# A two-layer pair-product kernel on one Trainium2 core: a new order of the slots, and the products with x1 in two row tiles of 64 rows, evicted two quarters at a time

## Chip, cores and metric

The kernel runs on one core of a Trainium2 chip. The metric is the device time of one execution in microseconds (us); lower is better. The time before is the median of three runs.

## What is computed

The input `x` has 2048 samples of 39 fields with 16 features each. There are two layers. Layer one is `x1[b,h,d] = sum over i,j of x[b,i,d] * x[b,j,d] * W0[i,j,h]` with 128 outputs h, layer two is `x2[b,h,d] = sum over i,j of x[b,i,d] * x1[b,j,d] * W1[i,j,h]`. The output is both layers summed over d, 256 numbers for each sample. The core of the reference:

```python
for W in (W0, W1):
    Hk = xk.shape[1]
    Wr = W.reshape(m, Hk, W.shape[-1])
    xk = jnp.einsum('bid,bjd,ijh->bhd', x0, xk, Wr)
    outs.append(xk)
return jnp.sum(jnp.concatenate(outs, axis=1), axis=-1)
```

## The kernel before, in words

**Numbers.** Every operand of a matmul is held as a high part in fp32r, and a low part that is the rest. A product of two such numbers is three matmuls that add into the same bank: high by high, low by high, high by low. ScalarE (ACT) makes the high parts by a Copy, VectorE (DVE) and GpSimd (POOL) make the low ones by a subtraction.

**Groups and chunks.** The 2048 x 16 columns are cut into 64 groups of 512 columns (32 samples). Eight groups are a chunk, so there are 8 chunks. The index `g` is a group, `gi` its place in its chunk, `j` the chunk. Chunk 0 and the last are written out, those between run in a loop of two chunks. Even and odd chunks store `gh` and `gl` in two different layouts, so that chunk j can overwrite the block that chunk j-1 has been read from.

**Layer one of a group.** SyncE (SP) loads x as the left factor (`xs`, 256 KB) and six slots of right factors (`xr`, 1536 KB, one transfer), each into one of two buffers. The products of slots 0, 2, 3, 5 are DVE's (L551), those of 1, 4 POOL's (L639). ACT rounds each to `fh` (L415), DVE (L555) or POOL (L644) subtracts to `fl`. PE adds three matmuls of 512 columns for each slot into `acc` (`main`, L329 to L331), and a seventh, FULL, for squares (L324). The products and roundings of group g+1 are made in the period in which PE works on group g.

**Layer two.** `x1_out` copies `acc` to SBUF (L436), `fill_turn` transposes it by four 128-column operations (L339), and L447 and L564 split the result into `x1th` and `x1tl`. The small matrix x1 x x of each sample is made by `g_tile` (L342 to L356) for a quarter (8 samples, 128 rows of (sample, feature)): the moving operand `xbd` is block diagonal, 8 samples by 40 columns, so each of three matmuls has 128 rows and 320 columns. Seven eighths of `xbd` are zeros. Two banks of `pg` take turns. ACT evicts each quarter as `gh` (L455, 128x320), DVE then as `gl` (L569). At the end of 8 groups `final` (L358 to L370) contracts 39 rows of gh and gl with `w1` in 39 x 3 matmuls of 256 columns; they are spread over the next chunk by `EARLY_ROWS` and `LATE_ROWS`.

**Order on PE in a period** (`chunk`, L372): early rows of `final`, quarters 2 and 3 of group g-2's place (`gi - 2`), slots 0, 1, 2, the transposes of g-1, slots 3, 4, late rows of `final`, slot 5, quarters 0 and 1 of g-1, FULL. In the first group of a chunk there are no rows of `final`, in the second 5, in the others 6 (5 in the last).

**Order on SP** (L273 to L293): when the products 4 and 5 of g are made, xs and xr of g+2; then `blocks`: eight small transfers that write the block diagonal (L264, SBUF to SBUF), after quarter 3 of g-2 is done; every second group the pair rows `xp`; then `xdr` of g+2. SP issues all transfers, one after another in program order. In chunk 0 it also loads w1 in 10 pieces into `outs`, each after POOL has split the one before.

**Start.** `w0a_raw` and `w0b_raw` lie in the second `xr` buffer, so `xr` of group 1 is loaded after the weights are split (L303, L304). PE waits for all weights (L395) before its first matmul.

Of the kernel before, what the change touches and what calls it, by code (L numbers as in the profile page):

```python
# [18 lines left out]
NT = 6  # L19
# [8 lines left out]
BQ = P // D  # L28
GB = GC // D
# [14 lines left out]
NW = 4  # L44
PIECES = -(-M // NW)
EARLY_ROWS = (0, 0, 2, 3, 3, 3, 3, 3)
LATE_ROWS = (0, 5, 3, 3, 3, 3, 3, 2)


def rows_of(gi, late):  # L50

    r0 = sum(EARLY_ROWS[:gi]) + sum(LATE_ROWS[:gi])
    if late:
        r0 += EARLY_ROWS[gi]
    return range(r0, r0 + (LATE_ROWS if late else EARLY_ROWS)[gi])


def pieces_of(gi):

    extra = PIECES - CB  # L60
    return range(gi + min(gi, extra), gi + 1 + min(gi + 1, extra))
# [41 lines left out]
def build(nc, xa, xb, xd, xpairs, w0a, w0b, w1, ident, out):  # L103
    with ExitStack() as ctx:
# [28 lines left out]
        xbd = sb("xbd", [P, 2, NQ, 2, BQ, MI], F32R)  # L133
# [4 lines left out]
        pg = ps("pg", [P, 2, GC])  # L138
# [3 lines left out]
        xr_flat = xr[:, 1, :, :].rearrange("p s c -> p (s c)")  # L142
        nw0 = len(ORDER) * H

        w0a_raw = xr_flat[:, 0:nw0]
        w0b_raw = xr_flat[:, nw0:2 * nw0]

        w0_in = sem("w0_in")
# [4 lines left out]
        xbd_zero = sem("xbd_zero")  # L153
        w1_in = sem("w1_in")
# [3 lines left out]
        xr_in = [sem("xr_in0"), sem("xr_in1")]  # L158
# [24 lines left out]
        outs_dma = sem("outs_dma")  # L183

# [19 lines left out]
        def wait_high(eng, g, t):  # L204
            eng.wait_ge(high_done, NT * g + t + 1)
# [7 lines left out]
        def g_at(g_buf, odd, gi, q):  # L213


            bs = slice(q * BQ, (q + 1) * BQ)
# [9 lines left out]
        def g_psum(odd, q):  # L226
            if odd:
                return pg[:, q % 2, 0:BQ * MI].rearrange("p (b i) -> p i b", b=BQ)
            return pg[:, q % 2, 0:BQ * MI].rearrange("p (b u r) -> p u r b", b=BQ, r=IB)
# [4 lines left out]
        def _(sp):  # L234
# [3 lines left out]
            def load_right(j, gi):  # L238
                sp.dma_start(xr[:, gi % 2, :, :], xb[CB * j + gi]).then_inc(xr_in[gi % 2], 16)
# [6 lines left out]

            def w1_load(p):
                n = min(NW, M - NW * p)
                if p:
                    sp.wait_ge(w1_ready, p)  # L250
                sp.dma_start(outs[:, :, :].rearrange("p a b -> p (a b)")[:, 0:n * H],
                             w1[:, NW * p * H:(NW * p + n) * H])\
                  .then_inc(w1_in if p < PIECES - 1 else outs_dma, 16)

            def blocks(g, gi, first):
                sp.wait_ge(xd_low, g + 1)
                if first and gi < 2:
                    sp.wait_ge(xbd_zero, 1)
                else:
                    sp.wait_ge(g_done, NQ * (g - 1))  # L260
                s = gi % 2
                for b in range(BQ):
                    rows = slice(D * b, D * b + D)
                    sp.dma_start(xbd[rows, s, :, :, b, :].rearrange("p q s i -> p (q s) i").bitcast(F32),  # L264
# [8 lines left out]
            def chunk(j, first, last):  # L273
                for gi in range(CB):
                    g = CB * j + gi
                    if not (last and gi + 2 >= CB):
                        wait_product(sp, g, 4)
                        wait_product(sp, g, 5)
                        load_x(j, gi + 2)
                        load_right(j, gi + 2)  # L280
                    blocks(g, gi, first)
                    if gi % 2 == 0 and not (last and gi + 2 >= CB):
                        sp.wait_ge(sq_ready, CP * j + gi // 2 + 1)
                        load_pair(CP * j + gi // 2 + 1)
                    if not (last and gi + 2 >= CB):
                        sp.wait_ge(xd_low, g + 2)
                        load_xd(g + 2)
                    if first:
                        for p in pieces_of(gi):
                            if p + 1 < PIECES:  # L290
                                w1_load(p + 1)
                    if gi == CB - 1 and not first:
                        send(j - 1)  # L293

            sp.dma_start(w0a_raw, w0a).then_inc(w0_in, 16)
            sp.dma_start(w0b_raw, w0b).then_inc(w0_in, 16)
            load_x(0, 0)
            load_right(0, 0)
            load_xd(0)
            load_pair(0)  # L300
            load_x(0, 1)
            sp.dma_start(idn[:, :], ident).then_inc(ident_in, 16)
            sp.wait_ge(w0_ready, 2)  # L303
            load_right(0, 1)  # L304
            w1_load(0)
            sp.wait_ge(xd_low, 1)
            load_xd(1)
            chunk(0, True, False)
            with sp.Fori(1, NCH - 1) as j:
                chunk(j, False, False)  # L310
            chunk(NCH - 1, False, True)
# [4 lines left out]
        def _(pe):  # L316
            def main(j, gi, t, fresh):
                g = CB * j + gi
                if t == 0 and not fresh:
                    pe.wait_ge(x1_ready, g)  # L320
                if t == FULL:
# [12 lines left out]
            def fill_turn(g, fresh):  # L334
                pe.wait_ge(x1_ready, g + 1)
                if not fresh:
# [5 lines left out]
            def g_tile(j, gi, q, fresh):  # L342
# [399 lines left out]
```

## Time and profile before

| | |
|---|---|
| median of 3 runs | 660.48 us (659.22 to 661.25) |
| the profiled execution | 658.78 us |
| its span | 657.0 us (so 1.78 us lie around it) |
| mean granted TensorE clock | 0.948 of 2.4 GHz |
| PE matmul busy | 573.5 us, 87% |
| ACT, DVE, POOL busy | 481.6, 477.2, 472.6 us (73, 73, 72%) |
| share of the 16 DMA engines | 68.6%, mean 226 GB/s |

The profile is one execution. Engine rows give busy time, and the idle time before a group of instructions with what ended it. SP's transfers stand as `SPq` rows whose time is that of the issue alone; an issue is not counted as busy. Starts and times in timelines are in us; PE rows overlap, since the end of a matmul lies after the start of the next, so what a matmul costs in a packed stretch is the distance between two starts.

### The profile page before, as it was taken

The numbers are of one execution on the slowest core, as the hardware profiler recorded it, in microseconds if no ns is written. First come the engines' busy times: TensorE is split into PE (matmuls) and PEld (weight loads), VectorE is DVE, ScalarE is ACT, GpSimd is POOL, SyncE is SP. The second block draws the span as 40 slices with busy tenths as digits, with TensorE's granted clock in tenths as the row PEclk, the third lists the DMA queues.
The fourth block names the chain that finished last, engine by engine and source line by source line (L and its number), as shares of the span: only waits on it lengthen the run. The fifth ranks groups of instructions, "written<-read, shape, count | busy, mean of one in ns | idle before, by whom it ended". The sixth has DMA issues, their size and how long they took to land.

```text
span 657.0 us, 13101 instructions
## 1 busy us (share of the span) xinstructions
PE 573.5 (87%) x3176; PEld 498.3 (76%) x3176; DVE 477.2 (73%) x804; ACT 481.6 (73%) x982; POOL 472.6 (72%) x407
## 2 busy tenths in 40 slices
PE   0458778999979998899979997999989999899978
PEld 0247666888868987688968896789968898689968
DVE  4527777788887787688886886878886888878730
ACT  3448787878877887678876887778887788778830
POOL 5668987778866887578875888578876788778700
PEclk9878898899989999799988999899998999999989
DMA  5757888668886687677775776867787677876310
GB/s 217 275 159 233 266 265 260 225 201 269 263 279 190 223 265 269 194 239 254 250 255 196 262 247 204 261 231 219 251 272 250 198 243 257 280 251 216 93 26 17
DMA packets 109081, 148.23 MB, mean 226 GB/s; under 512 B 77648, under 2 KB 86096, under 8 KB 100816
## 3 DMA queue, kind: packets, MB, share of 16 engines
q1 hardware_dynamic: 109008, 147.37, 68.6%
q8 instruction: 32, 0.52, 0.3%
q14 instruction: 41, 0.34, 0.2%
HBM read 134.74 MB, written 2.10 MB: 208 GB/s over the span
## 4 chain that ended last, share of the span: by engine, by line
PE 57%; DVE 14%; issue 11%; ACT 8%; DMA 6%; POOL 1%; ACTq 1%; SPq 0%; DVEq 0%
PE acc L329 9%; PE acc L330 9%; PE acc L331 9%; DMA xr<-xb_dram 5%; PE pg L354 5%; PE fin L366 5%; PE fin L367 5%; PE fin L368 4%; PE pg L355 4%; PE pg L356 4%; DVE fl L555 3%; DVE gl L569 3%; ACT gh L455 3%; PE turn L339 3%; DVE fp L551 2%
## 5 line engine op out<-in xcount | busy, mean ns | idle before, releaser
L644 POOL TENSOR_TENSOR fl<-fs,fh 128x512 fp32r<-128x512 f32 x192 | 256.7, 1337 | 67.0 <-ACT fh L415 66.8
L569 DVE TENSOR_TENSOR gl<-pg,gh 128x320 fp32r<-128x320 f32 x256 | 114.5, 486 | 110.5 <-ACT gh L455 109.6
L329 PE MATMUL acc<-fh,w0h 128*128 128x512 f32 x384 | 163.7, 426 | 25.0 <-DVE w0q L615 16.4
L639 POOL TENSOR_TENSOR fs<-xr,xs 128x512 f32<-128x512 f32 x128 | 163.7, 1301 | 8.7 <-DMA xr<-xb_dram 6.0
L415 ACT ACTIVATE fh<-fp 128x512 fp32r<-128x512 f32 x192 | 115.0, 599 | 63.5 <-DVE fp L551 37.5
L330 PE MATMUL acc<-fh,w0l 128*128 128x512 f32 x384 | 156.7, 408 | 0.0
L331 PE MATMUL acc<-fl,w0h 128*128 128x512 f32 x384 | 156.1, 406 | 0.0
L555 DVE TENSOR_TENSOR fl<-fp,fh 128x512 fp32r<-128x512 f32 x192 | 132.1, 688 | 28.1 <-ACT fh L415 25.8
L415 ACT ACTIVATE fh<-fs 128x512 fp32r<-128x512 f32 x192 | 120.1, 626 | 24.3 <-PE acc L331 19.7
L551 DVE TENSOR_TENSOR fp<-xl,xr 128x512 f32<-128x512 f32 x192 | 127.4, 694 | 13.6 <-DMA xr<-xb_dram 10.0
L354 PE MATMUL pg<-xbd,x1th 128*128 128x320 f32 x256 | 88.0, 344 | 51.4 <-DVE gl L569 32.5
L455 ACT ACTIVATE gh<-pg 128x320 fp32r<-128x320 f32 x256 | 101.2, 431 | 31.3 <-PE pg L356 24.9
L354 PEld LDWEIGHTS pg<-xbd,x1th 128*128 128x128 f32 x256 | 50.5, 197 | 69.9 <-DVE gl L569 42.8
L329 PEld LDWEIGHTS acc<-fh,w0h 128*128 128x128 f32 x384 | 76.5, 199 | 35.5 <-DVE w0q L615 16.4
L366 PE MATMUL fin<-gh,w1h 128*128 128x256 f32 x312 | 89.0, 285 | 1.1 <-DVE gl L569 1.1
L331 PEld LDWEIGHTS acc<-fl,w0h 128*128 128x128 f32 x384 | 75.8, 197 | 18.3
L367 PE MATMUL fin<-gh,w1l 128*128 128x256 f32 x312 | 88.9, 285 | 0.0
L368 PE MATMUL fin<-gl,w1h 128*128 128x256 f32 x312 | 88.6, 284 | 0.0
L330 PEld LDWEIGHTS acc<-fh,w0l 128*128 128x128 f32 x384 | 76.6, 199 | 10.0
L355 PE MATMUL pg<-xbd,x1th 128*128 128x320 f32 x256 | 82.5, 322 | 0.0
L356 PE MATMUL pg<-xbd,x1tl 128*128 128x320 f32 x256 | 82.5, 322 | 0.0
L648 POOL TENSOR_TENSOR xdhl<-xdr,xdhl 128x160 fp32r<-128x160 f32 x64 | 34.1, 533 | 66.6 <-ACT xdhl L443 66.6
(35 smaller groups left out, 730.6 us busy)
## 6 DMA issues: line engine op xcount, KB each, us to landing
xr<-xb_dram SPq DMA_DIRECT2D x64, 1536.0 KB, 7.5
xs<-xa_dram SPq DMA_DIRECT2D x64, 256.0 KB, 2.9
xbd<-xdhl SPq DMA_DIRECT2D x512, 20.0 KB, 3.4
xp<-xpairs_dram SPq DMA_DIRECT2D x32, 256.0 KB, 2.7
xdr<-xd_dram SPq DMA_DIRECT2D x64, 80.0 KB, 2.4
outs<-w_dram SPq DMA_DIRECT2D x9, 256.0 KB, 2.9
out_dram<-outs SPq DMA_DIRECT2D x8, 256.0 KB, 2.8
xr<-w0a_dram SPq DMA_DIRECT2D x1, 512.0 KB, 3.3
```

The lines of the kernel that those rows point to most:

```text
L329: nc.tensor.matmul(acc[:, :], w0h[:, t, :], fh[:, t, :], start=t == 0, stop=False)
L330: nc.tensor.matmul(acc[:, :], w0l[:, t, :], fh[:, t, :], start=False, stop=False)
L331: nc.tensor.matmul(acc[:, :], w0h[:, t, :], fl[:, t, :], start=False, stop=False)\
L354: nc.tensor.matmul(o, x1th[:, q, :], xh, start=True, stop=False)
L366: nc.tensor.matmul(o, w1h[:, i, :], h, start=i == 0, stop=False)
L367: nc.tensor.matmul(o, w1l[:, i, :], h, start=False, stop=False)
L415: nc.scalar.activation(fh[:, t, :], f_at(t), COPY).then_inc(high_done, 1)
L551: nc.vector.tensor_tensor(f_at(t), xl[:, :], xr[:, gi % 2, t, :], ALU.mult).then_inc(prod_dve, 1)
L555: nc.vector.tensor_tensor(fl[:, t, :], f_at(t), fh[:, t, :], ALU.subtract).then_inc(low_dve, 1)
L569: nc.vector.tensor_tensor(g_at(gl, odd, gi, q), g_psum(odd, q), g_at(gh, odd, gi, q), ALU.subtract).then_inc(g_low, 1)
L639: nc.gpsimd.tensor_tensor(f_at(t), xr[:, gi % 2, t, :], xs[:, gi % 2, :], ALU.mult)\
L644: nc.gpsimd.tensor_tensor(fl[:, t, :], f_at(t), fh[:, t, :], ALU.subtract).then_inc(low_pool, 1)
```

## The change

- **Row tiles.** `g_pair` takes the place of `g_tile`. A quarter's 128 rows are cut into two halves of 64 rows (4 samples each), and `xbd` has 4 blocks rather than 8, so each matmul has 64 rows and 160 columns. The two halves write different banks of `pg`. A pair of quarters is 2 x 3 x 2 = 12 matmuls, and `pg` (2 banks) holds one pair, with samples 64 columns apart. The next pair waits until the one before is evicted.
- **Eviction.** L455 and L569 become two instructions of 128x640 a group, where there were four of 128x320.
- **PE's order:** pair 0 of g-2, slots 0 to 2, pair 1 of g-2, transposes of g-1, slots 3 to 5, five rows of `final` (four in a chunk's first group, which are the last rows of the chunk before the previous one), FULL. The orders of ACT, DVE and POOL follow.
- **SP's order:** `blocks` first, then `xr` of g+3 in three transfers of two slots (512 KB each), each as soon as the products that read those slots are made, and `xs` of g+3.
- **Start.** w0 comes in two parts, into other places, and PE waits for each when it first needs it. w1 is copied in HBM to `w1_copy` (7 pieces), then loaded to `w1l` (7 pieces) and split in place.

The host permutes the samples of x accordingly. The diff, cut to what the text speaks of:

```diff
-NW = 4
+NR = 2
+RT = P // NR
+BR = BQ // NR
+BU = 2 * BQ
+NPAIR = NQ // 2
+HIGH = (0, 1, 2, 4, 3, 5)
+W0_PART = 4
+W0_FROM = {0: 1, W0_PART: 2, FULL: 3}
+NW = 6
-EARLY_ROWS = (0, 0, 2, 3, 3, 3, 3, 3)
-LATE_ROWS = (0, 5, 3, 3, 3, 3, 3, 2)
+def rows_of(s):
+    return range(IB * (s - 1), min(IB * s, M))
...
-        xbd = sb("xbd", [P, 2, NQ, 2, BQ, MI], F32R)
+        xbd = sb("xbd", [P, 2, NQ, 2, BR, MI], F32R)
-        pg = ps("pg", [P, 2, GC])
+        pg = ps("pg", [P, BU, GC // BR // 2])
...
-            def load_right(j, gi):
-                sp.dma_start(xr[:, gi % 2, :, :], xb[CB * j + gi]).then_inc(xr_in[gi % 2], 16)
+            def load_right(j, gi, u):
+                sp.dma_start(xr[:, gi % 2, 2 * u:2 * u + 2, :], xb[CB * j + gi][:, 2 * u:2 * u + 2, :])\
+                  .then_inc(xr_in[u][gi % 2], 16)
...
+            def w1_move(p):
+                sp.dma_start(w1_copy[:, piece(p), :], w1[:, piece(p), :]).then_inc(w1_moved, 16)
...
-            def chunk(j, first, last):
+            def chunk(j, first, second, last):
                 for gi in range(CB):
                     g = CB * j + gi
-                    if not (last and gi + 2 >= CB):
-                        wait_product(sp, g, 4)
-                        wait_product(sp, g, 5)
-                        load_x(j, gi + 2)
-                        load_right(j, gi + 2)
-                    blocks(g, gi, first)
+                    blocks(g, gi, first, last and gi == CB - 1)
+                    if more3:
+                        wait_product(sp, g + 1, 0)
+                        wait_product(sp, g + 1, 1)
+                        load_right(j, gi + 3, 0)
+                    if gi % 2 == 0 and more2:
                         sp.wait_ge(sq_ready, CP * j + gi // 2 + 1)
                         load_pair(CP * j + gi // 2 + 1)
+                    if more3:
+                        wait_product(sp, g + 1, 3)
+                        load_right(j, gi + 3, 1)
+                    if first and gi < PIECES:
+                        w1_load(gi)
+                        if gi + 1 < PIECES:
+                            w1_move(gi + 1)
+                    if more3:
+                        wait_product(sp, g + 1, 4)
+                        load_x(j, gi + 3)
+                        wait_product(sp, g + 1, 5)
+                        load_right(j, gi + 3, 2)
+                    if more2:
                         sp.wait_ge(xd_low, g + 2)
                         load_xd(g + 2)
...
-            def g_tile(j, gi, q, fresh):
+            def g_pair(j, gi, u, fresh):
                 g = CB * j + gi
                 s = gi % 2
-                if q == 0:
+                if u == 0:
                     pe.wait_ge(x1t_low, g + 1)
                     pe.wait_ge(xbd_in[s], 16 * BQ * nth(j, gi))
-                if not (fresh and q < 2):
-                    pe.wait_ge(g_low, NQ * g + q - 1)
-                o = pg[:, q % 2, 0:BQ * MI]
-                xh = xbd[:, s, q, 0, :, :].rearrange("p b i -> p (b i)")
-                xlo = xbd[:, s, q, 1, :, :].rearrange("p b i -> p (b i)")
-                nc.tensor.matmul(o, x1th[:, q, :], xh, start=True, stop=False)
-                nc.tensor.matmul(o, x1th[:, q, :], xlo, start=False, stop=False)
-                nc.tensor.matmul(o, x1tl[:, q, :], xh, start=False, stop=True).then_inc(g_done, 1)
+                if not fresh:
+                    pe.wait_ge(g_low, NPAIR * g + u)
+                for q in (2 * u, 2 * u + 1):
+                    for n, (left, part) in enumerate(((x1th, 0), (x1th, 1), (x1tl, 0))):
+                        for t in range(NR):
+                            rows = slice(RT * t, RT * t + RT)
+                            b0 = BQ * t + BR * (q % 2)
+                            o = pg[:, b0:b0 + BR, 0:MI]
+                            last = nc.tensor.matmul(o, left[rows, q, :],
+                                                    xbd[rows, s, q, part, :, :],
+                                                    start=n == 0, stop=n == 2)
+                last.then_inc(g_done, 1)
...
+                    if not (first and gi < 2):
+                        g_pair(j, gi - 2, 0, first and gi == 2)
+                    main(j, gi, 0, fresh)
+                    main(j, gi, 1, fresh)
+                    main(j, gi, 2, fresh)
+                    if not (first and gi < 2):
+                        g_pair(j, gi - 2, 1, False)
+                    if not fresh:
                         fill_turn(g - 1, first and gi == 1)
...
+                    main(j, gi, 3, fresh)
+                    main(j, gi, 4, fresh)
+                    main(j, gi, 5, fresh)
+                    if gi and not first:
+                        final(j - 1, not odd, rows_of(gi), second)
+                    if not gi and not (first or second):
+                        final(j - 2, odd, rows_of(CB), False)
+                    main(j, gi, FULL, fresh)
```

## Rows read from the trace of the kernel before

**Rows 1.** The page: busy time of each engine, its share of the span
```profile
PE 573.5 (87%) x3176; PEld 498.3 (76%) x3176; DVE 477.2 (73%) x804; ACT 481.6 (73%) x982; POOL 472.6 (72%) x407
```

**Rows 2.** PE timeline (start, us, what): transposes of groups 0, 8 and 63
```profile
38.98 1.05 PE L339 MATMUL turn<-idn,x 128*128 128x128 f32 x4
...
122.04 0.60 PE L339 MATMUL turn<-idn,x 128*128 128x128 f32 x4
...
631.37 0.60 PE L339 MATMUL turn<-idn,x 128*128 128x128 f32 x4
```

**Rows 3.** Busy time by stretch: bounds, length, engines, PEclk, DMA share, GB/s
```profile
38.98:122.04 83.06, 63.24 (x282) 51.70 (x280) 57.66 (x99) 62.42 (x128) 65.32 (x56) 0.89 0.78 248
...
301.17:318.64 17.47, 17.47 (x107) 15.72 (x106) 14.24 (x26) 14.78 (x31) 14.37 (x12) 1.00 0.80 263
```

**Rows 4.** PE timeline of one group in the packed stretch, 301.17 to 309.92
```profile
301.17 0.60 PE L339 MATMUL turn<-idn,x 128*128 128x128 f32 x4
301.53 0.48 PE L329 MATMUL acc<-fh,w0h 128*128 128x512 f32 x1
301.84 0.40 PE L330 MATMUL acc<-fh,w0l 128*128 128x512 f32 x1
...
303.00 0.28 PE L366 MATMUL fin<-gh,w1h 128*128 128x256 f32 x1
...
304.08 0.39 PE L329 MATMUL acc<-fh,w0h 128*128 128x512 f32 x1
...
304.78 0.31 PE L354 MATMUL pg<-xbd,x1th 128*128 128x320 f32 x1
...
305.66 0.39 PE L324 MATMUL acc<-sq,w0q 128*128 128x512 f32 x1
...
309.92 0.60 PE L339 MATMUL turn<-idn,x 128*128 128x128 f32 x4
```

**Rows 5.** PE timeline at the start of a chunk: the waits
```profile
181.35 0.41 PE L354 MATMUL pg<-xbd,x1th 128*128 128x320 f32 x1 [0.63 <-DVE gl L569]
181.60 0.31 PE L355 MATMUL pg<-xbd,x1th 128*128 128x320 f32 x1
...
188.90 0.41 PE L354 MATMUL pg<-xbd,x1th 128*128 128x320 f32 x1 [1.79 <-DVE x1tl L564]
```

**Rows 6.** SP timeline: its issues in one group of the packed stretch
```profile
308.07 5.30 SPq L264 DMA_DIRECT2D xbd<-xdhl  x8
313.56 0.45 SPq L245 DMA_DIRECT2D xdr<-xd_dram  x1
314.36 0.34 SPq L236 DMA_DIRECT2D xs<-xa_dram  x1
314.88 0.33 SPq L239 DMA_DIRECT2D xr<-xb_dram  x1
316.81 1.23 SPq L264 DMA_DIRECT2D xbd<-xdhl  x2
```

**Rows 7.** SP timeline in chunk 0: the eight block transfers
```profile
36.66 5.92 SPq L264 DMA_DIRECT2D xbd<-xdhl  x8
```

**Rows 8.** Timeline of the start: first product, first matmul, FULL of group 0, group 1
```profile
10.62 0.70 DVE L551 TENSOR_TENSOR fp<-xl,xr 128x512 f32<-128x512 f32 x1 [4.35 <-DMA xr<-xb_dram]
...
22.72 1.30 DVE L551 TENSOR_TENSOR fp<-xl,xr 128x512 f32<-128x512 f32 x2 [4.62 <-DMA xr<-xb_dram]
...
34.97 0.80 PE L329 MATMUL acc<-fh,w0h 128*128 128x512 f32 x1 [8.61 <-ACT x L436]
```

**Rows 9.** ACT and DVE timelines: evictions of two quarters, and 512 columns
```profile
305.85 0.74 ACT L455 ACTIVATE gh<-pg 128x320 fp32r<-128x320 f32 x2
...
308.81 0.60 ACT L415 ACTIVATE fh<-fp 128x512 fp32r<-128x512 f32 x1 [0.34 <-PE acc L331]
...
636.82 0.49 DVE L569 TENSOR_TENSOR gl<-pg,gh 128x320 fp32r<-128x320 f32 x1 [1.28 <-ACT gh L455]
...
310.83 0.69 DVE L555 TENSOR_TENSOR fl<-fp,fh 128x512 fp32r<-128x512 f32 x1
```

More of the change, by code:

```diff
@@ L43, with piece @@
 ORDER = (*range(NT), FULL, FULL)
-NW = 4
-PIECES = -(-M // NW)
-EARLY_ROWS = (0, 0, 2, 3, 3, 3, 3, 3)
-LATE_ROWS = (0, 5, 3, 3, 3, 3, 3, 2)
[L50 to L61, printed above, removed]
+HIGH = (0, 1, 2, 4, 3, 5)
+NU = NT // 2
+W0_PART = 4
+W0_FROM = {0: 1, W0_PART: 2, FULL: 3}
+NW = 6
+PIECES = -(-M // NW)
+def rows_of(s):
+    return range(IB * (s - 1), min(IB * s, M))
+def piece(p):
+    return slice(NW * p, min(NW * p + NW, M))
 def pair_slots():
@@ L297, in _ @@
-            load_x(0, 0)
-            load_right(0, 0)
+                    if gi == 2 and not (first or second):
+                        send(j - 2)
+            w0_load(0)
+            load_x(0, 0)
+            load_right(0, 0, 0)
+            w0_load(1)
+            load_right(0, 0, 1)
+            load_right(0, 0, 2)
+            load_pair(0)
             load_xd(0)
-            load_pair(0)
             load_x(0, 1)
+            load_right(0, 1, 0)
             sp.dma_start(idn[:, :], ident).then_inc(ident_in, 16)
-            sp.wait_ge(w0_ready, 2)
@@ L311, in _ @@
-            chunk(NCH - 1, False, True)
+            wait_product(sp, 0, 4)
+            load_x(0, 2)
+            wait_product(sp, 0, 5)
+            load_right(0, 2, 2)
+            w1_move(0)
+            chunk(0, True, False, False)
+            chunk(1, False, True, False)
+            with sp.Fori(2, NCH - 1) as j:
+                chunk(j, False, False, False)
+            chunk(NCH - 1, False, False, True)
+            send(NCH - 2)
             send(NCH - 1)
@@ L335, in fill_turn @@
                 pe.wait_ge(x1_ready, g + 1)
-                if not fresh:
+                if fresh:
+                    pe.wait_ge(ident_in, 16)
+                else:
                     pe.wait_ge(x1t_low, g)
@@ L404, in _ @@
+            g_pair(NCH - 1, CB - 2, 0, False)
+            final(NCH - 2, False, rows_of(CB), False)
+            g_pair(NCH - 1, CB - 2, 1, False)
             fill_turn(NG - 1, False)
-            for q in range(NQ):
-                g_tile(NCH - 1, CB - 1, q, False)
-            final(NCH - 1, True, range(M))
+            for u in range(NPAIR):
+                g_pair(NCH - 1, CB - 1, u, False)
+            final(NCH - 1, True, range(M), False)
         @block.scalar
@@ L495, in chunk @@
                     if more:
-                        high(g + 1, 3, False)
                         xd_split(j, gi + 1, first and gi == 0)
                         high(g + 1, 4, False)
+                        high(g + 1, 3, False)
+                    if gi == 1 and not (first or second):
+                        final_out(j - 2)
+                    if first and 0 < gi <= PIECES:
+                        w1_high_part(gi - 1)
+                    if more:
+                        high(g + 1, 5, False)
@@ L530, in _ @@
-            chunk(NCH - 1, False, True, True)
+            chunk(0, True, False, False, False)
+            chunk(1, False, True, False, True)
+            with act.Fori(1, NCH // 2 - 1) as pair:
+                chunk(2 * pair, False, False, False, False)
+                chunk(2 * pair + 1, False, False, False, True)
+            chunk(NCH - 2, False, False, False, False)
+            chunk(NCH - 1, False, False, True, True)
+            x1_out(NG - 1, False)
             g_high_part(NCH - 1, CB - 2, 0, True, None)
@@ L614, in _ @@
-            dve.wait_ge(w0_sum, 2)
+            product(0, 0, 5, True)
+            dve.wait_ge(w0_sum, 3)
             nc.vector.tensor_tensor(w0q[:, :, :], last_lo, x1th[:, 0:2, :], ALU.add).then_inc(w0_ready, 1)
             low(0, 2)
-            product(0, 0, 5, True)
             low(0, 3)
             chunk(0, True, False, False)
-            with dve.Fori(0, NCH // 2 - 1) as pair:
+            chunk(1, False, False, True)
+            with dve.Fori(1, NCH // 2 - 1) as pair:
+                chunk(2 * pair, False, False, False)
@@ L675, in chunk @@
                         low(g + 1, 4)
-                    if gi == 3 and not first:
+                    if gi == 5 and not first:
                         first_out(j - 1, not odd)
-                    if first:
-                        for p in pieces_of(gi):
-                            w1_piece(p)
+                    if first and 0 < gi <= PIECES:
+                        w1_low_part(gi - 1)
             nc.gpsimd.memset(xbd[:, :, :, :, :, :].rearrange("p u q s b i -> p (u q s b i)").bitcast(F32), 0.0)\
```

284 lines of the change are left out of this document (127 added, 157 removed).

## The prediction, made before the changed kernel was run

> **What bounds the kernel now.** I read the page first: PE is the busiest engine, the other three lie at 72 or 73% [rows 1]. A share of the whole span says little here, so I then took the distance between the transposes of successive groups, one set in each period. The first set starts at 38.98, the ninth at 122.04, the last at 631.37 [rows 2]. So the span of 657.0 falls into 39.0 before the first set, 83.1 for the first 8 periods (10.4 each), 509.3 for the next 55 (9.26 each) and 25.6 behind the last.
>
> The busy time by stretch shows what holds each part. In the packed stretch in a chunk's middle PE is busy all of 17.47 us for two groups, at the full clock of 2.4 GHz, while ACT, DVE and POOL have 14.2 to 14.8 [rows 3]: PE's own work sets the 8.74 us of a group. In chunk 0 no engine is full (PE 63 of 83 us) and the clock is down to 0.89 [rows 3]. Between these, at the start of each chunk, PE waits for evictions and for `x1tl`: 0.63 and 1.79 us in one instance [rows 5]. That is why the mean is 9.26 and not 8.74.
>
> The timeline of the packed group gives PE's prices, from start to start [rows 4]: 512 columns 0.233 (304.08 to 304.78 for three), 256 columns 0.120 (303.00 to 304.08 for nine), 320 columns 0.147 (304.78 to 305.66 for six). The four transposes with the matmul behind them take 0.67 (301.17 to 301.84), so they cost 0.44. A period has 18 x 0.233 + 0.44 + 0.23 + 12 x 0.147 = 6.62 without rows of `final`, each of which costs 0.36. With 6 rows that is 8.78, with 5 it is 8.42; the trace has 8.75 [rows 4], so I take 8.38 with 5 rows. Of it the x1 products have 1.76, all else 6.62.
>
> SP's timeline is the view that matters next. Eight block transfers take 5.30 us to issue, then `xdr`, `xs` and `xr` until 315.21, and the next block starts at 316.81 [rows 6]. So SP works 7.14 of 8.74 us, with the pair rows every second group about 7.4, and idles 1.3 to 1.6.
>
> **The change, part by part.**
>
> *x1 products on PE.* 12 matmuls of 320 columns become 24 of 160, in pairs on two row halves. No row shows a row tile. If the halves overlap fully, and a pair costs what the shortest matmul in the trace does (a 128-column transpose, 0.44 / 4 = 0.11 [rows 4]), this is 12 x 0.11 = 1.32, a gain of 0.44. If nothing overlaps and each costs its columns (160 / 320 x 0.133 + 0.014 = 0.08), 1.92, a loss of 0.16. If each costs the 0.11 of a transpose, 2.64, a loss of 0.88. As an upper end each costs the 0.147 of today's [rows 4]: 3.53. There are four changes between whole array and halves in a period; each costs between nothing and 0.16, the part of a 320-column matmul (0.31) that now lies under the next (0.147) [rows 4]. I take 1.32 with 0.2 for the changes: PE 6.62 + 1.52 = 8.1 a period. The trace is nearest to this in that weight loads run ahead today at no cost.
>
> *Evictions.* ACT needs 0.74 for two quarters; from 320 columns (0.44, half of what a pair takes apart) to 512 (0.60) is 0.83 ns a column, so 640 take about 0.71. DVE has 0.49 and 0.69 [rows 9], so about 0.82. Each engine saves some 0.15 a group, which ends no wait. `pg` no longer alternates: pair 1 waits until pair 0 is evicted, 0.71 + 0.82 + 0.3 for the last matmul and the semaphores = 1.8, against 9 matmuls of slots 0 to 2, 2.1 us. Hidden by 0.3, if ACT and DVE come in time; behind that wait are the transposes and all of x1's split. I add nothing, and keep 0 to 0.3 a group for the range.
>
> *The order.* `final` stands before FULL, 5 rows in every period, so the chunk's first period no longer runs without it and its operands are made half a period before. The waits of rows 5 go: the mean can come down to what the fullest queue needs.
>
> *SP.* The blocks stay. `xr` becomes three issues: two more at the distance of `xs` to `xr`, 0.52, or with a wait that is already met up to 0.56: +1.1. With 0.2 before the next block (313.37 to 313.56 [rows 6]) SP needs 7.3 + 1.1 + 0.2 = 8.6, and I take 8.65 with the added product waits. That is above PE's 8.1. SP now runs more than a period ahead, so its waits are mostly met, but its throughput isn't changed by that. So **SP's issue queue becomes the bound, at 8.65 us a group**, and what PE gains by row tiles is hidden behind it. 55 x 8.65 = 476.
>
> *Start.* The first product waits until 10.62 for all of w0 and `xr`, 2.8 MB; now it needs 1.25 MB. Group 1's product waits until 22.72 for a transfer that was issued only after the weights' split, and its first matmul comes at 34.97 after w1 pieces on ACT [rows 8]. Both go: group 0's matmuls from about 10, FULL at 17, group 1 from 20, its transposes at about 23 (from 39).
>
> *Chunk 0.* The w1 loads no longer hold SP until POOL has split the piece before. But SP has two more issues a period (+1.0), and blocks take 5.92 there [rows 7], 0.6 more: 8.65 + 1.0 + 0.6 is 10.2; I take 10 for seven periods and 8.65 for the eighth, 79 (from 83). The added copy of w1 in HBM, 2.6 MB, adds to a DMA share of 0.78 [rows 3]; in that stretch at its 248 GB/s it is up to 10 us of transfer, beside which SP's queue is about as long. Both ends stay in the range, as plus or minus 10.
>
> *Tail.* The same 39 rows, waits of the same kind: 26.
>
> Sum: 23 + 79 + 476 + 26 = 604, and 1.8 around the span: 605.6. The profiled execution of before, 658.8, is 1.7 below the median of the runs, 660.5; I don't correct for it and say **605**. With 8.45 to 8.85 a period and the 10 us of the start this forecast by itself spans 590 to 622.
>
> **Rivals.** All have 128 us outside the 55 periods, and 1.8 around.
>
> (a) *Weights in line.* Each half's weights are loaded one after the other, and 24 matmuls cost 0.11 each: PE 6.62 + 2.64 = 9.26 is the bound. 128 + 509 + 1.8 = **639**. For it: four transposes are the only short matmuls here, and cost 0.11 although 128 columns at 2.4 GHz are 0.053 [rows 4]. Against it: they may be slow as transposes. The Trainium skill, "TensorE: Matmul & The Clock Gate", section "LDWEIGHTS", says that a load takes its 128 columns at 1.2 GHz, 107 ns, however few rows it has; an estimate by it gives the same 2.6 us. By that rule, and the trace's 0.11 agrees with it, halves cost as much as whole loads.
>
> (b) *The other side: the array drains at each change.* As (a), and all four changes cost 0.16 (rows 4): PE 6.62 + 2.64 + 0.64 = 9.9, 128 + 544 + 1.8 = **674**. It decides from a period of 9.62, that is x1 products of 3.0 us, 0.125 for each of the 24 matmuls, changes included. Today a matmul starts while the one before is still under way, at every place of rows 4; nothing there changes the tiling, so the trace is silent. The Trainium skill, "TensorEngine Tiling (Array Packing)", section "Key Properties", states that changing the mode drains TensorE. By that rule the drain is paid at every pair, and no row here shows it.
>
> (c) *SP is not the bound.* If issues come cheaper once DMA queues are less in step, PE at 8.0 is: 128 + 440 + 1.8 = **570**. Against it: the block issues took 5.3 here and 5.9 in chunk 0 [rows 6, 7], never less.
>
> (d) *The tiles don't overlap*, so the change doesn't do what it says: PE 6.62 + 1.92 = 8.54, below SP's 8.65. The time is that of the forecast; it is counted there.
>
> (e) *Pair 1 waits for its bank* 0.3 or more a group behind late evictions, since ACT in a period with squares has nearly 8 us of work: 8.95, **622**.
>
> **Chances.** Forecast 0.45, (a) 0.22, (b) 0.12, (c) 0.15, (e) 0.06. A range of 570 to 650 leaves out (b), half of (c) and a little of (a), about 0.2. A measurement of this kernel can tell 0.3%, 2 us, from no change. Slower: (b), 0.12; in between 0.02; faster 0.86.
>
> **What the profile would show.** Right: transposes 8.6 to 8.7 apart all through the chunks with no 11 or 12 at their starts; SP's timeline without idle time; PE waiting 0.3 to 0.6 a period for `xbd` or products; first transposes at 23, the ninth near 102. Starts of the two halves a few ns apart, and 12 matmuls in about 0.7 us, would show the overlap. Wrong: PE packed at 9.2 or more (a, b), with the gap at the first 64-row matmul telling (b); SP idle with periods at 8.0 (c); or gaps before pair 1 with DVE `gl` as releaser (e).

## The result, and the profile after

The changed kernel takes **801.79 us** (median of 4 runs, 801.28 to 805.32) against 659.85 for the kernel before on the same occasion: a ratio of 1.217, 95% interval 1.212 to 1.222. The forecast was 605 us with a range of 570 to 650: wrong in sign and far outside. The profiled execution has a span of 803.1 us. Below, times are medians of all runs of a kernel, and ratios leave out the runs that were over 1.5% slower than its fastest.

The page of the changed kernel: busy time, then who ended the chain of waits (by engine, by line).

```profile
PE 634.3 (79%) x3944; PEld 514.1 (64%) x3944; DVE 460.6 (57%) x678; ACT 460.2 (57%) x852; POOL 463.5 (58%) x404
...
PE 35%; DMA 29%; SPq 13%; ACT 11%; issue 8%; DVE 2%; ACTq 1%; POOL 1%; DVEq 0%; POOLq 0%
DMA xdr<-xd_dram 28%; SPq L277 8%; PE acc L368 7%; PE pg L398 6%; PE acc L369 6%; PE acc L370 6%; ACT fh L462 4%; SPq L243 3%; PE fin L413 3%; PE fin L414 2%; PE fin L415 2%; ACT xl L469 2%; DVE fp L590 2%; ACT gh L502 2%; ACT x L483 2%
```

Against [rows 1], no engine is nearer to full than before, and DVE and ACT do less in all (460 us each, from 477 and 482). 28% of the chain is the landing of one small transfer, `xdr`, of 80 KB. The waits say the same (engine and line, waited for, us in total, times, longest).

```profile
ACT xdhl L490 <- DMA xdr<-xd_dram: 145.9, 36, 6.9
DVE gl L608 <- ACT gh L502: 125.7, 119, 4.6
PE acc L368 <- ACT x L483: 110.9, 33, 6.7
```

ACT waits 145.9 us for `xdr`; PE waits 110.9 for the copy of `acc` that stands behind it on ACT. The last DMA part of the page shows how long the transfer lands, in the last column; in the kernel before it was 2.4.

```profile
xs<-xa_dram SPq DMA_DIRECT2D x64, 256.0 KB, 5.3
xbd<-xdhl SPq DMA_DIRECT2D x512, 20.0 KB, 2.4
...
xdr<-xd_dram SPq DMA_DIRECT2D x64, 80.0 KB, 5.9
```

The transposes of groups 0, 8 and 63, as in [rows 2]:

```profile
28.27 0.60 PE L380 MATMUL turn<-idn,x 128*128 128x128 f32 x4
...
128.39 0.66 PE L380 MATMUL turn<-idn,x 128*128 128x128 f32 x4
...
775.41 0.66 PE L380 MATMUL turn<-idn,x 128*128 128x128 f32 x4
```

| part | before | forecast | measured |
|---|---|---|---|
| to the first transposes | 39.0 | 23 | 28.3 |
| first 8 periods | 83.1 | 79 | 100.1 |
| the other 55, each | 9.26 | 8.65 | 11.76 |
| behind the last | 25.6 | 26 | 27.7 |

Of the 199 us between the forecast's sum for the span (604) and the span, 171 are in the 55 periods. These aren't alike: in the middle of the trace one of 8.7 us follows one of 15 us. Two of them, read in four timelines. First SP's:

```profile
322.64 6.00 SPq L277 DMA_DIRECT2D xbd<-xdhl  x8
329.00 0.34 SPq L243 DMA_DIRECT2D xr<-xb_dram  x1
329.59 0.34 SPq L247 DMA_DIRECT2D xp<-xpairs_dram  x1
330.18 0.33 SPq L243 DMA_DIRECT2D xr<-xb_dram  x1
330.76 0.33 SPq L240 DMA_DIRECT2D xs<-xa_dram  x1
331.34 0.33 SPq L243 DMA_DIRECT2D xr<-xb_dram  x1
331.86 0.33 SPq L250 DMA_DIRECT2D xdr<-xd_dram  x1
...
346.48 2.04 SPq L277 DMA_DIRECT2D xbd<-xdhl  x2
```

The chain that ended last, for the transfer itself:

```profile
331.86 6.47 DMA xdr<-xd_dram
```

ACT's timeline, where it lands:

```profile
332.43 0.60 ACT L494 ACTIVATE x1th<-turn 128x512 fp32r<-128x512 f32 x1
338.43 0.34 ACT L490 ACTIVATE xdhl<-xdr 128x160 fp32r<-128x160 f32 x1 [5.39 <-DMA xdr<-xd_dram]
338.67 0.61 ACT L462 ACTIVATE fh<-fs 128x512 fp32r<-128x512 f32 x1
339.19 0.58 ACT L462 ACTIVATE fh<-fp 128x512 fp32r<-128x512 f32 x1
339.67 0.62 ACT L462 ACTIVATE fh<-fs 128x512 fp32r<-128x512 f32 x1
340.19 0.59 ACT L469 ACTIVATE xl<-xs 128x512 f32<-128x512 f32 x1
340.71 0.58 ACT L483 ACTIVATE x<-acc 128x512 f32<-128x512 f32 x1
```

PE's, which waits for the last of these:

```profile
341.51 0.79 PE L368 MATMUL acc<-fh,w0h 128*128 128x512 f32 x1 [4.72 <-ACT x L483]
...
342.96 0.63 PE L368 MATMUL acc<-fh,w0h 128*128 128x512 f32 x1
...
344.24 0.63 PE L368 MATMUL acc<-fh,w0h 128*128 128x512 f32 x1
...
345.54 0.45 PE L398 MATMUL pg<-xbd,x1th 64*128 64x160 f32 x4
```

It is a closed loop. Pair 1 is done, the semaphore `g_done` rises, SP starts the blocks (322.64) and behind them four or five large loads, and only then `xdr` (331.86, 9.2 us later). That lands 6.5 us later (338.4), behind 2.0 MB of loads here, 1.8 MB in a group without pair rows. ACT, which works in order, has stood still for 5.4 us; it then does `xdhl`, three roundings, `xl` and the copy of `acc` (2.9 us). PE waits for that copy, does slots 0 to 2 and pair 1 (5.0 us), and `g_done` rises again (346.48). 9.2 + 6.5 + 3.1 + 5.0 = 23.8 us for two periods, 11.9 each, and 11.76 is the mean. PE's part costs 5.0 and not the 3.2 of the short period before: behind its wait of 4.7 us the granted clock is 0.52 (1.2 GHz) and the slots are 1.28 to 1.45 us apart, in the short period it is 1.00 and they are 0.69 to 0.80 apart.

### The profile page after: what moved, and what is told of

The parts are those of the page before. It is cut to its first block, busy times and chain, and to the rows that moved or that the text cites. A ratio compares the mean times of both kernels' runs of the same rounds, so it can differ in the third digit from the quotient of the medians.

```text
span 803.1 us, 14074 instructions
## 1 busy us (share of the span) xinstructions
PE 634.3 (79%) x3944; PEld 514.1 (64%) x3944; DVE 460.6 (57%) x678; ACT 460.2 (57%) x852; POOL 463.5 (58%) x404
## 4 chain that ended last, share of the span: by engine, by line
PE 35%; DMA 29%; SPq 13%; ACT 11%; issue 8%; DVE 2%; ACTq 1%; POOL 1%; DVEq 0%; POOLq 0%
DMA xdr<-xd_dram 28%; SPq L277 8%; PE acc L368 7%; PE pg L398 6%; PE acc L369 6%; PE acc L370 6%; ACT fh L462 4%; SPq L243 3%; PE fin L413 3%; PE fin L414 2%; PE fin L415 2%; ACT xl L469 2%; DVE fp L590 2%; ACT gh L502 2%; ACT x L483 2%
## 5 line engine op out<-in xcount | busy, mean ns | idle before, releaser
L368 PE MATMUL acc<-fh,w0h 128*128 128x512 f32 x384 | 189.2, 493 | 125.1 <-ACT x L483 110.9
L608 DVE TENSOR_TENSOR gl<-pg,gh 128x640 fp32r<-128x640 f32 x128 | 105.6, 825 | 126.0 <-ACT gh L502 125.7
L369 PE MATMUL acc<-fh,w0l 128*128 128x512 f32 x384 | 173.2, 451 | 0.0
L370 PE MATMUL acc<-fl,w0h 128*128 128x512 f32 x384 | 171.7, 447 | 0.0
L502 ACT ACTIVATE gh<-pg 128x640 fp32r<-128x640 f32 x128 | 90.0, 703 | 69.6 <-PE pg L398 69.6
L398 PEld LDWEIGHTS pg<-xbd,x1th 64*128 64x128 f32 x1024 | 83.1, 201 | 55.8 <-issue 46.3
L398 PE MATMUL pg<-xbd,x1th 64*128 64x160 f32 x1024 | 108.4, 303 | 9.6 <-DVE x1tl L603 5.2
L490 ACT ACTIVATE xdhl<-xdr 128x160 fp32r<-128x160 f32 x64 | 21.8, 341 | 146.1 <-DMA xdr<-xd_dram 145.9
L369 PEld LDWEIGHTS acc<-fh,w0l 128*128 128x128 f32 x384 | 87.5, 228 | 14.6
L413 PEld LDWEIGHTS fin<-gh,w1h 128*128 128x128 f32 x312 | 63.6, 204 | 35.9 <-issue 25.3
```

The costliest lines, as they stand in the source:

```text
L368: nc.tensor.matmul(acc[:, :], w0h[:, t, :], fh[:, t, :], start=t == 0, stop=False)
L369: nc.tensor.matmul(acc[:, :], w0l[:, t, :], fh[:, t, :], start=False, stop=False)
L370: nc.tensor.matmul(acc[:, :], w0h[:, t, :], fl[:, t, :], start=False, stop=False)\
L398: last = nc.tensor.matmul(o, left[rows, q, :], xbd[rows, s, q, part, :, :], start=n == 0, stop=n == 2)
L413: nc.tensor.matmul(o, w1h[:, i, :], h, start=i == 0, stop=False)
```

## The experiments

Theory **A** is this loop. Rival **B**: the row tiles and their evictions. Rival **C**: `xr` in thirds lands late.

**1. `xdr` issued right behind the blocks.**

```diff
                     blocks(g, gi, first, last and gi == CB - 1)
+                    if more2:
+                        sp.wait_ge(xd_low, g + 2)
+                        load_xd(g + 2)
...
-                    if more2:
-                        sp.wait_ge(xd_low, g + 2)
-                        load_xd(g + 2)
```

> The changed kernel, with one edit: SP issues the load of xdr for g+2 right behind the eight block transfers, ahead of xr and xs. Theory A (a loop over two periods: g_done of pair 1, blocks 6.0 us, five other issues to 9.2 us, 6.5 us landing of xdr behind 1.8 MB, ACT's split and four more operations 2.8 us, PE's slots 0 to 2 and a pair 5.0 us, g_done again: 23.8 us): xdr is issued 6.4 us behind g_done and lands in about 2.4 us as before, the loop falls to 16 to 17 us for two periods, under SP's own 9.0 a period (9.65 with pair rows, 8.3 without, read from the changed kernel). Then 55 x 9.0 + 128 + 2 = 625 us, waits of ACT for xdr gone. Theory B (the row tiles and their evictions stall PE): unchanged, near 800. Theory C (xr in thirds lands later and starves the products): near 800, with waits of DVE and POOL for xr.

Measured: **665.42 us**, ratio to before 1.012 (1.006 to 1.019). Three lines moved past five loads give back 136 of 142 us. The DMA part of the page, with the landing time last:

```profile
xdr<-xd_dram SPq DMA_DIRECT2D x64, 80.0 KB, 2.2
```

SP's timeline, with `xdr` ahead of the large loads:

```profile
292.66 5.79 SPq L277 DMA_DIRECT2D xbd<-xdhl  x8
298.63 0.45 SPq L250 DMA_DIRECT2D xdr<-xd_dram  x1
299.44 0.34 SPq L243 DMA_DIRECT2D xr<-xb_dram  x1
```

`xdr` lands 2.2 us behind its issue, and of ACT's 145.9 us of waits for it 1.4 are left. B and C fall as causes of these 136 us, since the tiles and the thirds are all still there. But 625 was expected, and the 55 periods are 9.52 each, so something else binds behind the loop.

**2. `xdr` in two buffers, its load one group further ahead, its place kept.**

```diff
-        xdr = sb("xdr", [P, NQ, MI])
+        xdr = sb("xdr", [P, 2, NQ, MI])
...
-                    if more2:
+                    if more3:
                         sp.wait_ge(xd_low, g + 2)
-                        load_xd(g + 2)
+                        load_xd(j, gi + 3)
```

> The changed kernel, with xdr in two buffers and the load of g+3 where that of g+2 stood, at the end of SP's round: the order of issues and the landing time stay. Theory A: the same 24 us of loop are now spread over three periods, 8 us each, so it no longer binds: about 625 us although xdr still takes 5 to 6 us to land. A rival within A, that it is the order on the queue and not the distance ahead that matters: stays above 750. Theories B and C: near 800.

Measured: **652.25 us**, ratio 0.988 (0.983 to 0.992). `xdr` still takes 6.1 us to land, and ACT waits for it once, 0.2 us. So its late landing costs nothing by itself; it costs inside a loop with one buffer. The 625 us expected were missed by 27, as in experiment 1.

**3. The kernel before with row tiles only** (`g_pair`, `xbd` with 4 blocks, evictions of 640 columns, its own orders).

```diff
-                        for q in (2, 3):
-                            g_tile(j, gi - 2, q, False)
+                        g_pair(j, gi - 2, 1, False)
...
-                        for q in (0, 1):
-                            g_tile(j, gi - 1, q, first and gi == 1)
+                        g_pair(j, gi - 1, 0, first and gi == 1)
```

> The kernel before with its own orders, and only the row tiles: twelve matmuls of 64 rows and 160 columns for two quarters, one eviction of 640 columns. Theory A: the loss is not in the tiles, so within some per cent of before. A pair and the changes of tiling around it took 1.0 us in the changed kernel against 0.88 for six full matmuls, 0.24 us a group more, and pair 1 waits for its banks, as only FULL and the early rows lie between the pairs: 0.5 to 1.5 us a group. So 680 to 750 us, with DVE gl as the releaser of pg. Theory B: near 800.

Measured: **687.39 us**, ratio 1.046 (1.039 to 1.053), in the range expected. Steady periods are 9.28, from 8.74. In PE's timeline pair 0 starts at 306.60, FULL at 307.43, and pair 1 has to wait for both banks:

```profile
307.43 0.50 PE L330 MATMUL acc<-sq,w0q 128*128 128x512 f32 x1
309.16 0.45 PE L363 MATMUL pg<-xbd,x1th 64*128 64x160 f32 x4 [0.18 <-DVE gl L572]
```

In the whole run PE waits 53.9 us for this eviction at the pairs, from 32.5 in the kernel before.

**4. Experiment 1 with the full array** (`NR = 1`: 128 rows, 320 columns, six matmuls for a pair, same order and evictions).

```diff
-NR = 2
+NR = 1
...
-        pg = ps("pg", [P, BU, GC // BR // 2])
+        pg = ps("pg", [P, BU, 2 * GC // BU])
```

> The first kernel of this set, with the full array in place of the row tiles: 128 rows, 8 blocks, 320 columns, three matmuls a quarter, still two quarters to an eviction of 640 columns. If SP's queue binds at 9.0 us a period, the same time as the first to 1%, PE idle more. If PE binds, 0.2 to 0.3 us a group less than the first, since 12 short matmuls with the changes took 1.0 us and six long ones 0.88: 12 to 20 us faster. If the row tiles gain, it is slower than the first by up to 0.44 x 64 = 28 us.

Measured: 665.95 us, ratio 1.010 (1.000 to 1.021), the same as experiment 1 within the intervals. Something other than PE binds. Theory **D**: SP's issue queue.

**5. Two of SP's five other issues moved to ACT** (on experiment 2).

```diff
-                        load_x(j, gi + 3)
-                        load_right(j, gi + 3, 2)
...
                         high(g + 1, 5, False)
+                    if not (last and gi + 3 >= CB):
+                        h = gi + 3
+                        nc.scalar.dma_start(xs[:, h % 2, :], xa[CB * j + h]).then_inc(xs_in[h % 2], 16)
+                        nc.scalar.dma_start(xr[:, h % 2, 4:6, :], xb[CB * j + h][:, 4:6, :])\
+                          .then_inc(xr_in[2][h % 2], 16)
```

> As xd_two_buffers, and the loads of xs and of the last third of xr for g+3 are issued from ACT's queue behind the rounding of slot 5, where they need no wait. SP's round there is 8.2 us without pair rows and 9.6 with, a mean of 9.1 when it isn't stalled; five transfers besides the blocks take 0.58 from start to start. Theory D (SP's issue queue binds what is left): SP falls by 1.15 us to about 7.9, PE's own 8.7 becomes the bound, 128 + 55 x 8.75 + 2 = 611 us. Rival E (the DMA queues are full, 150 MB and 128,000 packets at a share of 0.7 to 0.8, and transfers land late whoever issues them): within 1.5% of 652. Rival F (ACT is full): it takes 0.7 us more of ACT and becomes slower, 660 or more.

Measured: **637.95 us**, ratio 0.970 (0.963 to 0.978), from 0.988. That is 14 us from 652.25 (11 by the ratios), a third of the 41 expected. It is below the 642 that rival E allowed at the least, and F, slower, didn't come either. The edit does two things at once: SP has two issues fewer, and `xs` lands in 3.0 us rather than 5.3, so that ACT's wait for it, 33.2 us in experiment 2, is gone.

**6. The same with the full array.**

> As the run before, with the full array in place of the row tiles. If PE is the bound there, its group falls by the difference of 12 short matmuls with their changes of tiling (1.0 us a pair) and six long ones (0.88): 0.24 to 0.3 us a group, 15 us faster than the run before, 595 us. If SP, DMA or ACT bind, the same within 0.5%.

Measured: 634.27 us, ratio 0.961 (0.956 to 0.965); the intervals of 5 and 6 overlap. The 15 us expected of the full array didn't come; the medians differ by 3.7.

**7. `xr` in two transfers** (on experiment 2; slots 0 to 3, slots 4 and 5).

```diff
-                    if more3:
-                        wait_product(sp, g + 1, 0)
-                        wait_product(sp, g + 1, 1)
-                        load_right(j, gi + 3, 0)
...
                     if more3:
+                        wait_product(sp, g + 1, 1)
                         wait_product(sp, g + 1, 3)
-                        load_right(j, gi + 3, 1)
+                        load_right(j, gi + 3, 0)
```

> As xd_two_buffers, with xr in two transfers (slots 0 to 3, slots 4 and 5), the first issued when product 3 is made. One issue fewer on SP, 0.55 us of 9.1. Theory D: 25 to 30 us faster than 652, 625 us. Rival E: the bytes are the same and the packets fewer by 128 a group (8 KB ones in place of two of 4 KB), within 1% of 652.

Measured: **635.28 us**, ratio 0.965 (0.959 to 0.970), 17 us under experiment 2 (15 by the ratios), where D expected 25 to 30 and E within 1%. Experiments 5 and 7 both take issues off SP and gain, with the same bytes; that speaks for D. Experiment 7 also has fewer packets, so its gain alone wouldn't settle it; 5 has as many as 2. In both ACT waits less for `xs` (12.1 us in experiment 7), which SP issues behind other transfers; no run takes an issue off SP and leaves the landing of `xs` as it was, so the two aren't told apart.

Experiment 2 itself holds a comparison. In the changed kernels chunk 1 is written out, and chunks 2 to 6 run in a loop, with the same transfers in the same order. Busy time of its chunk 1 and of its loop (columns as in [rows 3]):

```profile
112.16:181.73 69.57, 68.75 (x495) 56.74 (x494) 57.58 (x85) 56.48 (x104) 56.84 (x50) 1.00 0.80 258
181.73:566.60 384.87, 358.38 (x2467) 292.52 (x2465) 281.42 (x421) 284.65 (x525) 282.75 (x246) 0.96 0.74 235
```

Written out, SP's issues besides the blocks are 0.47 us apart, a period is 8.70, PE is busy 99% and the DMA engines move 258 GB/s. In the loop the issues are 0.58 apart, a period is 9.62 and they move 235 GB/s. So E, full DMA queues, isn't what holds the loop back. D fits: 4.5 issues at 0.11 less make a round of 9.0 one of 8.5, below PE's 8.7 (an estimate). Why an issue takes longer in the loop is not shown.

**8. The kernel before with `xdr` behind `xr`.**

```diff
                         load_right(j, gi + 2)
+                    if not (last and gi + 1 >= CB):
+                        sp.wait_ge(xd_low, g + 1)
+                        load_xd(g + 1)
                     blocks(g, gi, first)
...
-                    if not (last and gi + 2 >= CB):
-                        sp.wait_ge(xd_low, g + 2)
-                        load_xd(g + 2)
```

> The kernel before with one edit: the load of xdr goes from behind the pair rows to behind xs and xr of the next round, ahead of the blocks: about 1 us later in SP's order, and behind 1.8 MB in the DMA queue. In the kernel before it landed 2.4 us behind its issue and some 4 us before ACT split it; behind xr it should land 7 to 8 us behind. Theory A: ACT, which works in order, stalls on it 1 to 3 us in each group, with PE behind it: 720 to 800 us, and waits of ACT xdhl for DMA xdr on top of the list. If the order of the queue is harmless: 660.

Measured: **718.15 us**, ratio 1.089 (1.082 to 1.096), just under the expected range. The waits:

```profile
PE pg L352 <- DVE gl L567: 76.1, 35, 10.2
ACT xdhl L441 <- DMA xdr<-xd_dram: 66.5, 40, 4.8
```

The landing time goes from 2.4 to 6.6 us, and a wait comes up that the kernel before doesn't have. It is fifth in the list, not on top; what grows with it is PE's wait for evictions (76.1 us, from 32.5), which stand behind `xdhl` on ACT. One misplaced 80 KB load costs the old kernel 58 us. Why it costs less here than the 136 us of experiment 1 isn't tested: between `g_done` and `xdr` stand the blocks and two or three issues here, four or five there.

**9. Experiment 7 with the full array.**

> As xr_two_transfers (635 us), with the full array. In that run the steady periods read 8.7, PE's own time with tiles; with the full array they were 8.6 in act_issues_full_array. If PE binds in most periods, 0.1 us x 55 = 5 us faster, 630 us; by the price of the pairs alone (1.0 against 0.88 us, twice a group) it would be 13 us, 622. If SP or the landing of xs binds: the same within 0.5%.

Measured: 632.97 us, ratio 0.957 (0.950 to 0.963). The same as 7 within the intervals.

**10. The same, and `xs` issued from ACT, the last third of `xr` behind `xdr`.**

```diff
-                        load_x(j, gi + 3)
...
                         high(g + 1, 3, False)
+                    if not (last and gi + 3 >= CB):
+                        h = gi + 3
+                        nc.scalar.dma_start(xs[:, h % 2, :], xa[CB * j + h]).then_inc(xs_in[h % 2], 16)
```

> As two_transfers_full_array, and the load of xs for g+3 is issued from ACT's queue behind the rounding of slot 3, with the last third of xr behind xdr on SP. SP has one issue fewer, 0.58 us, and xs lands 3.0 us behind its issue (as in the runs where ACT issued it) instead of 5.4. If waits for xs (13% of the chain in xd_two_buffers) are what is left: 610 to 620 us, periods at 8.4 to 8.6. If ACT's added 0.4 us a group costs as much: the same within 0.5%.

Measured: **621.46 us**, ratio 0.944 (0.939 to 0.950). This is the fastest of all, 5.6% under the kernel before, and just above the 610 to 620 expected. It too changes both SP's issues and the landing of `xs` (4.1 us, from 5.4). The busy time by stretch of its 55 periods, and of 17 us in the middle (columns as in [rows 3]):

```profile
104.37:588.72 484.35, 470.09 (x2737) 412.26 (x2736) 387.51 (x567) 381.86 (x709) 380.95 (x329) 1.00 0.79 247
270.00:287.00 17.00, 17.00 (x101) 14.90 (x100) 13.76 (x22) 13.86 (x27) 14.85 (x13) 1.00 0.86 267
```

PE is busy 97% of the 55 periods, at the full clock; in the kernel before it was 479.8 of 509.3 us (94%), at 0.97. Apart from one period of 9.5 to 9.8 at each chunk's start and one of 11.9, the periods take 8.2 to 9.1 us. Now PE is the bound nearly everywhere.

**11. The changed kernel with the full array, nothing else.**

> The changed kernel as it is, with the full array in place of the row tiles, nothing else. Theory A: the loop over xdr binds and holds only two pairs' worth of PE (the pair that gives g_done), so 800 us within 2%. Theory B (the tiles and their changes cost the time): near 660.

Measured: 820.97 us, ratio 1.250 (1.240 to 1.259), 2.4% above the changed kernel, and the intervals of the two don't overlap. So B falls: without the tiles the kernel isn't faster but slower, and by a little more than the 2% that A allowed. In the slow period of this kernel the six matmuls of a pair take 0.27 us each, at the lower clock. That is 1.6 us, where the tiles take 1.5, a difference in the right direction and far from 19 us. What makes the rest stays open.

**12. Experiment 10 with the row tiles back.**

> As xs_from_act_full_array (621 us), with the row tiles back: the pair of kernels in which least else binds. Steady periods read 8.60 there; the tiles' steady period is 8.68 to 8.70 in every run so far. So 5 to 6 us slower if most periods are PE's, 627 us. By my price of a pair, 1.0 us against 0.88, twice a group, it would be up to 13 us slower, 634. If the tiles gain at all, it is under 621.

Measured: 626.24 us, ratio 0.948 (0.945 to 0.952), 0.4% above experiment 10 by the ratios, with overlapping intervals. The mean of 55 periods is 8.90 against 8.81 in the two profiles. Now the price of a pair can be read. PE's timeline with tiles (x4 is four records put together, two pairs of halves):

```profile
283.01 0.39 PE L365 MATMUL acc<-fl,w0h 128*128 128x512 f32 x1
283.33 0.45 PE L393 MATMUL pg<-xbd,x1th 64*128 64x160 f32 x4
283.62 0.28 PE L393 MATMUL pg<-xbd,x1tl 64*128 64x160 f32 x2
283.73 0.39 PE L393 MATMUL pg<-xbd,x1th 64*128 64x160 f32 x4
283.95 0.28 PE L393 MATMUL pg<-xbd,x1tl 64*128 64x160 f32 x2
284.16 0.66 PE L375 MATMUL turn<-idn,x 128*128 128x128 f32 x4
284.57 0.48 PE L363 MATMUL acc<-fh,w0h 128*128 128x512 f32 x1
```

and with the full array:

```profile
286.04 0.39 PE L365 MATMUL acc<-fl,w0h 128*128 128x512 f32 x1
286.27 0.45 PE L393 MATMUL pg<-xbd,x1th 128*128 128x320 f32 x2
...
287.14 0.60 PE L375 MATMUL turn<-idn,x 128*128 128x128 f32 x4
287.50 0.48 PE L363 MATMUL acc<-fh,w0h 128*128 128x512 f32 x1
```

From the end of slot 2's stream (its last start plus 0.23) to the transposes: 0.92 with tiles, 0.87 without. From the transposes to slot 3: 0.41 and 0.36. So pair 1 costs 0.10 more with tiles, which is the difference of the steady periods, 8.70 and 8.60. Inside, the halves do run together, two matmuls of 160 columns in 0.11 us (283.62 to 283.73, and 283.73 to 283.95 for four). Three such steps are 0.33 a quarter, the three full ones are 0.44: a gain of 0.11, 0.22 a pair. Two changes of tiling eat it: 0.09 before the first half (283.24 to 283.33), some 0.07 in the first quarter (0.40 in place of 0.33), 0.1 before the transposes and 0.05 in them, 0.31 in all. As for pair 0, its length doesn't count in either kernel, since slot 0 waits for ACT's copy of `acc` (FULL, then slot 0). PE's timeline with tiles:

```profile
279.82 0.39 PE L358 MATMUL acc<-sq,w0q 128*128 128x512 f32 x1
...
281.07 0.49 PE L363 MATMUL acc<-fh,w0h 128*128 128x512 f32 x1
```

and with the full array:

```profile
282.83 0.40 PE L358 MATMUL acc<-sq,w0q 128*128 128x512 f32 x1
...
284.08 0.49 PE L363 MATMUL acc<-fh,w0h 128*128 128x512 f32 x1
```

FULL to slot 0 is 1.25 us in both. FULL takes 0.40 to its end, the copy 0.6, and what PE does meanwhile is free.

## Why the prediction was wrong

**SP, the step that failed.** "SP now runs more than a period ahead, so its waits are mostly met": the text counted what SP issues and not in which order the things come that others wait for. `xdr` has one buffer and is loaded only one group ahead, as before, while `xr` moved further ahead. `xdr` went from the place right behind the blocks to the last place, behind five issues and 1.8 MB. The prediction has no line that prices that move, nor one for ACT, which stands in order behind the landing. SP isn't a queue with a throughput here but a part of a loop of 23.8 us in two periods: 11.76 us a period, where the sum had 8.65. Experiment 1 undoes the move and takes 136 us away; experiment 8 puts `xdr` behind the large loads in the old kernel, and costs 58.

What was known would have given it. [Rows 6] have 5.30 us for the blocks; four or five issues at 0.52 to 0.56 follow, 8 us to the issue of `xdr`; `xr` before landed in 7.5 us by the page; ACT's four copies and PE's slots with a pair are 2.5 and 3 us. That is 21 us for two periods, above twice 8.65.

**SP's own size.** Its round was forecast at 8.65 (from 7.3, where [rows 6] gave 7.4). In the loop chunks, with no stall, it is 9.65 with pair rows and 8.3 without, a mean of 9.0: the blocks mostly took 5.1 to 6.0 us, not 5.3, and the other issues are 0.58 apart, not 0.52 to 0.56. That SP binds behind the loop over `xdr` is borne out in part: with that loop gone the full array changes nothing (experiment 4), fewer issues gain 14 to 17 us (5, 7), and where the issues are closer together the periods fall to 8.7 (chunk 1 of experiment 2). It isn't the whole: the mean is 9.52 and 9.38, not 9.0, in experiments 1 and 2, and in experiment 1 ACT waits 50.9 us for `xs`, which lands in 5.5 us where it did in 2.9. Issued by ACT it lands in 4.1, and another 11.5 us go (10); how much of that is the landing and how much the issue taken off SP stays open.

**Row tiles.** 1.32 us of matmuls a group was right: 12 x 0.11. The 0.2 for four changes of tiling was too low, since the two around pair 1 alone cost 0.31. So the gain of 0.24 a group became a loss of 0.10. The Trainium skill, "TensorEngine Tiling (Array Packing)", section "Key Properties", has a change of mode drain the array; the time lost around pair 1 in experiment 12, about 0.15 us a change, agrees with it. Rival (a) fell: halves on different rows don't load their weights in line, as two matmuls with their loads take 0.11 us together. That speaks against the 2.6 us that the prediction estimated from the Trainium skill, "TensorE: Matmul & The Clock Gate", section "LDWEIGHTS", by adding up the loads of both halves; the length that the section gives for a single load isn't tested by it.

**Rival (b)** named the right side, slower, with the wrong mechanism: its steady 9.9 us a period by drains is in no run; with tiles and SP unloaded it is 8.7 (experiment 12). **(c)** had PE at 8.0 there. Of the 0.7 between, pair 1's changes are 0.3, and FULL to slot 0 takes 1.25 us, where FULL and 12 halves in pairs at 0.11 are 0.9. **(e)** was small: with slots 0 to 2 between the pairs, PE waits 1.7 us for evictions in the whole changed kernel. Experiment 3, without these slots, shows what the order is good for. The evictions were priced right: 0.70 and 0.82, for a forecast of 0.71 and 0.82.

**The start.** First transposes 28.3 for 23. The forecast put every load at the full rate, but product 0 waits until 10.10, since it stands behind the second w0 part on DVE, and the first matmul comes at 12.46 (forecast 10). Then group 0's matmuls are mostly 0.43 us apart and not 0.233, so FULL starts at 21.42, not 17. Chunk 0's 100 for 79 goes with the same loop; with the loop gone it is 75 to 86.

**The order of `final`.** The waits at chunk starts [rows 5] went for the most part: periods of 10.1 to 13.7 us there in the kernel before are 9.5 to 9.8 in experiment 10. The forecast had them at 8.65 too; what makes the rest stays open.

## What to carry to other kernels

When a step is moved in the order of a queue, follow the smallest transfer in it too: who waits for it, whether that engine works in order, how many buffers it has, and whether its wait closes a loop back to the queue. Then add up the loop and divide by the groups it spans, before counting any engine's busy time. A load that is needed soon goes ahead of the large ones, or gets one buffer more; either alone took 136 to 150 us away here. Row tiles pay only where enough matmuls stand between two changes: at 0.11 us gained a quarter and 0.31 lost for two changes, that is three quarters or more (an estimate). With two quarters they came out 0.1 us a group behind, which the total can't tell from even.

## What the runs showed of the hardware

- An 80 KB load lands 2.2 to 2.5 us behind its issue (medians of a run) when it is issued right behind the small block transfers (the kernel before, experiments 1 and 3), and 5.1 to 6.6 when it is issued right behind 1 to 2 MB of loads (experiments 2, 5, 7, 8, 10).
- Two matmuls of 64 rows and 160 columns on different row halves, weight loads included, take 0.11 us together at 2.4 GHz (experiment 12), and 0.21 at 1.2 GHz (316.76 to 316.97 in the changed kernel's PE timeline, granted clock 0.50).
- An issue on SP costs 0.33 us, 0.58 from start to start with a wait that is met, in the loop chunks; in the written-out chunk 1 of experiment 2 issues are 0.47 apart. A block transfer of 16 rows by 8 pieces takes 0.64 to 0.75 us, as a mean of eight.
- Issued from ACT's queue beside SP's, `xs` (256 KB) landed in 2.9 to 3.0 us and the last third of `xr` (512 KB) in 4.5 to 4.6 (experiments 5 and 6), and the total falls by 14 us rather than rises.
